# Two weight pieces beside each group of rows in a graph layer with a mixture of experts: where the pieces are loaded, split and read

## The reference, cut to what matters

```python
W = zeros((256, 256)).at[src, dst].set(edge_weight)      # the last edge with these indices wins
x = x + layernorm(x) @ W
xn = layernorm(layernorm(x)) * gamma + beta
logits = xn @ Wr + br                                    # 8 experts
w_full = softmax over the two largest logits, 0 elsewhere
for e in range(8):
    h = gelu(xn @ W1[e] + b1[e])                         # 256 -> 512
    y = y + (h @ W2[e] + b2[e]) * w_full[..., e]         # 512 -> 256
x = x + y
```

## Time and profile before

| what | us |
|---|---|
| three timed runs: lowest, median, highest | 1133.49, 1137.07, 1141.1 |
| the profiled execution, its own time | 1138.41 |
| its span in the profile (first to last recorded instruction) | 1136.7 |
| busy in the span: PE, DVE, ACT, POOL | 949.9, 759.6, 622.8, 590.5 |
| start of the first W2 load beside a group that waits (end of DVE's group 3) | 146.25 |
| first load of `zin` | 465.91 |

### The profile page before, as it was taken

One profiled execution on the slowest core, in us unless ns is written; L12 is line 12 of the kernel. 1 busy time (PEld: TensorE's weight loads), 2 busy tenths in 40 slices (PEclk: granted clock), 3 DMA queues, 4 the chain that ended last, 5 costly groups with the idle time before them and its releaser, 6 DMA issues. The chain is left out here.

```text
span 1136.7 us, 25491 instructions
## 1 busy us (share of the span) xinstructions
PE 949.9 (84%) x6852; PEld 896.3 (79%) x6853; DVE 759.6 (67%) x2345; ACT 622.8 (55%) x1309; POOL 590.5 (52%) x457
## 2 busy tenths in 40 slices
PE   2557876676667757699999999999999999999992
PEld 1236765565556547699999999999999999999992
DVE  6957856655555657377777777777777777777771
ACT  1025744434444442376676766766766766767661
POOL 3100664554545577044755566556556566565663
PEclk9886966666666665699999999999999999999997
DMA  3024444444444466544655455454454554554542
GB/s 93 1 70 103 160 161 140 147 145 140 165 142 149 159 217 194 173 78 82 93 88 91 76 93 89 78 93 84 83 93 80 88 93 75 93 89 79 93 72 32
DMA packets 96200, 121.45 MB, mean 107 GB/s; under 512 B 15240, under 2 KB 73776, under 8 KB 96028
## 3 DMA queue, kind: packets, MB, share of 16 engines
q0 software_dynamic: 39904, 53.56, 26.9%
q1 hardware_dynamic: 55944, 66.55, 19.7%
q10 hardware_dynamic: 308, 0.85, 0.2%
HBM read 51.93 MB, written 68.98 MB: 106 GB/s over the span
## 5 line engine op out<-in xcount | busy, mean ns | idle before, releaser
L565 POOL DMA_INDIRECT out_dram<-ysb,yid x210 | 379.5, 1807 | 295.8 <-ACT ysb L1342 141.8
L734 PE MATMUL psum<-xh,w1s 128*128 128x256 f32 x1680 | 311.6, 286 | 0.0
L549 POOL DMA_INDIRECT slots<-arena_z,pos x196 | 195.0, 995 | 222.0 <-DVE pos L1024 164.3
L734 PEld LDWEIGHTS psum<-xh,w1s 128*128 128x128 f32 x1680 | 257.7, 189 | 0.0
L747 PE MATMUL psum<-w2h,hl 128*128 x840 | 237.8, 283 | 0.0
L747 PE MATMUL psum<-w2l,hh 128*128 x840 | 237.5, 283 | 0.0
L747 PE MATMUL psum<-w2h,hh 128*128 x840 | 236.4, 281 | 0.0
L734 PE MATMUL psum<-xl,w1s 128*128 128x256 f32 x840 | 235.8, 281 | 0.0
L1161 DVE TENSOR_TENSOR hl<-hact,hh 128x512 fp32r<-128x512 f32 x210 | 145.6, 693 | 87.5 <-ACT hh L1214 87.5
L646 PE MATMUL psum<-table,arena_s 128*128 128x256 f32 x392 | 135.4, 504 | 60.5 <-DVE arena_s L1051 60.5
L1325 ACT ACTIVATE hact<-psum,b1T 128x256 f32<-128x256 f32 x420 | 174.6, 467 | 14.2 <-PE psum L734 2.7
(11 more groups left out here) (182 smaller groups left out, 1173.3 us busy)
## 6 DMA issues: line engine op xcount, KB each, us to landing
zin<-slots SPq DMA_DIRECT2D x105, 260.0 KB
arena_x<-in_x_dram SPq DMA_DIRECT2D x14, 512.0 KB, 6.0
out_dram<-arena_s SPq DMA_DIRECT2D x14, 512.0 KB, 4.5
wst_new<-in_L_ffn_W_dram SPq DMA_DIRECT2D x20, 256.0 KB, 3.1
arena_x<-in_x_dram SPq DMA_DIRECT2D x13, 384.0 KB, 7.0
out_dram<-arena_s SPq DMA_DIRECT2D x13, 384.0 KB
out_dram<-ysb,yid POOLq DMA_INDIRECT x210, 4.2
slots<-arena_z,pos POOLq DMA_INDIRECT x196, 2.6
```

The costliest lines, as they stand in the source:

```text
L549: pool.indirect_dma_start(slots[:, :], bass.IndirectOffsetOnAxis(ap=pos[b][0:n, k, s:s + 1], axis=0), zg[b][0:n, s, :], None).then_inc(sen ...
L565: pool.indirect_dma_start(out[:, :], bass.IndirectOffsetOnAxis(ap=yid[u % MB][:, n:n + 1], axis=0), ysb[u % YB][:, n, :], None, compute_op ...
L734: last = nc.tensor.matmul(bank[2 + 2 * b + q][:, m * PAIR:(m + 1) * PAIR], w1s[b][:, w, k, hb * P:(hb + 1) * P], xs[b][:, k * PAIR:(k + 1) ...
```

## The change

Two pieces stand beside each of the groups 2 to 13, so 24 beside groups and 8 behind the last one. In SP the two pieces of group g + 1 are loaded behind `turn_over(g)`, and their buffers' former users are the pieces of group g. In ACT the two `high` stand inside group g, between `exp_gap` and the z side. In DVE the two `low` of group g stand at its end. In PE the bias products of W1 pieces (groups 10 to 13) stand between the ranks and `edge_product(g, 1)`; five more come behind the last ranks and ahead of the count, and the last three behind `tables_ready`. The halves of each bias sum go to columns of their own in bank 6, and DVE adds both.

```diff
-BESIDE = 12
+BESIDE = 2 * (GROUPS - FIRST_BESIDE)
-MIDDLE = PIECES + WBUFS
+MIDDLE = BESIDE + WBUFS
+def beside(g):
+    return range(2 * (g - FIRST_BESIDE), 2 * (g - FIRST_BESIDE) + 2) if FIRST_BESIDE <= g < GROUPS else ()
...
 # SP
-            for n in range(2):
+            for n in beside(FIRST_BESIDE):
                 load_w(n)
             for g in range(2, GROUPS - 3):
                 turn_over(g, g % 2)
-                load_w(g)
+                for n in beside(g + 1):
+                    load_w(n)
             turn_over(GROUPS - 3, 1, full=False)
-            load_w(GROUPS - 3)
+            for n in beside(GROUPS - 2):
+                load_w(n)
             turn_over(GROUPS - 2, 0, load=False)
+            for n in beside(GROUPS - 1):
+                load_w(n)
             sp.wait_ge(xT_mm, NP * GROUPS)
-            for n in range(BESIDE, BESIDE + WBUFS):
+            for n in range(BESIDE, MIDDLE):
                 load_w(n)
...
 # PE
+            def bias(n):
+                e, k = (n - PIECES) // KD, n % KD
+                pe.wait_ge(stage_in[WBUF[n]], 16 * turn_of(n) + 16)
+                for hb in range(KH):
+                    at = G * E + E * KH * k + KH * e + hb
+                    last = nc.tensor.matmul(bank[6][:, at:at + 1], wst[WBUF[n]][:, hb * P:(hb + 1) * P], bet[:, k:k + 1], start=True, stop=True)
+                last.then_inc(w_read, 1)
...
                 if older:
                     ranks(g - 2)
+                for n in beside(g):
+                    if n >= PIECES:
+                        bias(n)
                 if x_side:
                     edge_product(g, 1)
...
             ranks(GROUPS - 1)
+            for n in range(BESIDE, MIDDLE):
+                bias(n)
             pe.wait_ge(routed, GROUPS)
...
-            for n in range(PIECES):
...
             pe.wait_ge(tables_ready, 1)
+            for n in range(MIDDLE, WHOLE):
+                bias(n)
...
 # DVE
-                if g > FIRST_BESIDE:
-                    low(g - FIRST_BESIDE - 1)
+                for n in beside(g):
+                    low(n)
...
-            for n in range(BESIDE - 1, MIDDLE):
+            for n in range(BESIDE, MIDDLE):
                 low(n)
...
-            v.tensor_tensor(b1T[:, :], bank[7][:, 0:E * KH], b1raw[:, :], ALU.add).then_inc(bias_ready, 1)
+            t.then(v.tensor_tensor(b1raw[:, :], bank[6][:, G * E:G * E + E * KH], b1raw[:, :], ALU.add))
+            v.tensor_tensor(b1T[:, :], bank[6][:, G * E + E * KH:G * E + 2 * E * KH], b1raw[:, :], ALU.add).then_inc(bias_ready, 1)
...
 # ACT
                 if older:
                     exp_gap(g - 2)
+                for n in beside(g):
+                    high(n)
                 if z_side:
...
                 group(g, g % 2)
-                high(g - FIRST_BESIDE)
```

More of the change, by code:

```diff
@@ L441, in _ @@
             sp.dma_start(out[(TILES - 1) * P:N, :], x1g[0:LAST, G - 1, :]).then_inc(x1_out[1], 16)
-            for n in range(BESIDE + WBUFS, WHOLE):
+            for n in range(MIDDLE, WHOLE):
                 load_w(n)
```

## The result

The changed kernel takes 1104.25 us (median of 4 runs, 1099.19 to 1108.13) beside 1139.09 us for the kernel before on the same chip (4 runs, 1133.49 to 1143.2). The ratio is 0.9686, 95% interval 0.9653 to 0.9719: 34.8 us faster, where 47 had been forecast. The profiled execution took 1105.56 us, its span is 1103.8 us.

A forecast was written before the change was run, and what follows sets the result against it. Loads of x queued on SP behind waiting weight loads were taken to bound the groups. 130.1 + 7 x 21.0 + 4 x 23.6 = 371.5, plus 47.0, puts `zin` at 418.5, 47.4 us earlier: 1091.0 us profiled, 1090 median, range 1062 to 1110.

The forecast's parts named there:

- the stall of x: Front-stage groups: DVE's 76.3 us wait for x, whose loads queue behind weight loads on SP, falls to under 10.
- R of group 2: R is when DVE finishes a group's router; for group 2, two high parts ahead of the z side give 130.1.
- z side begins (groups 3 to 9): ACT starts its z side after both high parts, 5.2 to 5.9 us behind the previous group's router end.
- cycle of groups 3 to 9: Weight wait, z-side chain of 14.2 us and clock loss: 21.0 us a group (19.4 to 22.7).
- cycle of groups 10 to 13: PE's W1 bias products ahead of `edge_product(g, 1)`, 1.75 us a piece, make 23.6 us a group.
- R of group 13 to `zin`: End of the front stage, from the last router's end through count, tables and fillers to the load of `zin`: 47.0 us.
- `zin` to the end: The pair stage, which the change does not touch, stays within 2 us of 668.
- Both signs asked for: DVE's wait for x under 10 us; ACT's z side 5.2 to 5.9 us behind the router's end.
- The clock: PE's z chain after its pause, groups 3 to 9: half clock costs 2.6 us; half of that, 1.3, was taken.
- a sign of being wrong: The forecast is wrong if, among other signs, cycles of groups 3 to 9 are under 19 or over 23 us.
- Weights that land late: Rival: weight loads compete with POOL's sends; at 10 us of landing the kernel takes 1163 us; slower had chance 0.05.
- Hidden weights: Rival: splits and POOL set the pace, 18.3 us for all eleven groups, 1050 us; hidden or nearly so, chance 0.12.

The follow-up runs named there:

- e1: The kernel before, with each weight load one group later on SP, behind the loads of x it had held up: 1052.28 us, ratio 0.9232.
- e2: The changed kernel with ACT's high parts moved from ahead of the z side to the end of its group: 1051.59 us, ratio 0.9234.
- e4: The changed kernel with five unused matmuls on PE ahead of the z transposes of groups 3 to 9: 1090.68 us, ratio 0.9567.
- e13: The changed kernel with an unused 128x112 tile declared last in the front stage, so no pair-stage tile moves: 1104.01 us, ratio 0.9694.
- e6: The changed kernel with the count put ahead of the five bias products behind the last group: 1106.58 us in one run.
- e3: e2 with PE's bias products also moved, behind the third piece of the z side and ahead of the last logits: 1051.02 us, ratio 0.9218.
- e11: The changed kernel with an unused 128x112 tile declared behind first_gelu, which moves pair-stage tiles: 1091.39 us, ratio 0.9558.
- e12: The kernel of e3 with the same unused tile in the same place as in e11: 1037.54 us, ratio 0.9106.
- e9: The kernel of e3 with a POOL memset of an otherwise unused tile behind each of 196 sends: 1052.4 us, ratio 0.9229.
- e10: The changed kernel with the same memset and tile as e9, behind each of POOL's 196 sends: 1090.11 us, ratio 0.9552.

## Why the prediction was right, and where it was off

The direction and the mechanism were right, and the range held the time, 6 us inside its upper end: the stall of x goes, ACT's wait for the weights takes its place, and the lost time shows in the front stage. The forecast gain was 12.6 us too large. The profiled execution took 1105.56 us against a sum of 1091.0, and the 14.6 us between them fall on these steps (spans add up to 14.5):

| Step | Predicted | Measured | Share of the error |
|---|---|---|---|
| R of group 2 | 130.1 | 131.32 | +1.2 |
| z side begins (groups 3 to 9) | R + 5.2 to 5.9 | R + 5.49 (mean of 7, 4.84 to 6.31) | 0 |
| cycle of groups 3 to 9 | 21.0 | 22.7 (mean of 7, 21.1 to 25.9) | +11.7 |
| cycle of groups 10 to 13 | 23.6 | 23.1 (mean of 4) | -2.1 |
| R of group 13 to `zin` | 47.0 | 46.8 | -0.2 |
| `zin` to the end | 670.8, as before | 674.7 | +3.9 |

**The stall and the new wait.** Both signs asked for are there: DVE's wait for x is gone and ACT's z side begins, in the mean, where it was put. e1 showed that the order of the queue was the cause of the stall, and e2 that the high parts ahead of the z side, with their wait and what hangs on it, were all that kept groups 3 to 9 of the changed kernel from 17 us. POOL waited 53.4 us in 12 times for its places after the first (136.3 less 82.9), 4.4 us a group, inside the 2 to 5 us forecast.

**The clock, the step that failed.** I took half of 2.6 us for the PE work behind the pause. In group 5 the time from the z side to `add(2)` is 192.01 - 183.61 = 8.4 us, where it was 5.6 in group 3 of before: 2.8 us, not 1.3. All seven products `edge_product(g, 2)` of groups 3 to 9 took 3.36 to 3.76 us; e4 filled the pause, brought four of seven back to 1.97 us, and got 13.6 us of the time back. In groups 4 to 9 it is 16.8 us in the mean from the z side to the next R, 2.6 more than the 14.2 of before (1.7 to 3.1 one by one): in the mean the full price. The Trainium skill (TensorE: Matmul & The Clock Gate, HAM oscillation) has a PE that waits for a DMA in every round of a loop start every round cold. By that rule the full price would have been the forecast, and the trace agrees, though PE waits here for ACT, and only ACT for the DMA. With 2.6 us in place of 1.3 the cycle is 22.3, and seven of them take up 9.1 of the 11.7 us. Two of the seven cycles, 25.9 and 23.2 us, are over the 23 that I had named as a sign of being wrong; their mean is not. The rest is group 3, with 25.9 us where the other six have 22.1 in the mean. Its loads left at 132.03 over 1.82 us, not 0.97, and its z side began only at 137.63, R + 6.3; more of it is the clock again, which was 0.50 from 140 to 157 us, so that all the rest of the group ran at 1.2 GHz (in group 5 it was 0.50 from 188.1 to 191.9 and 0.87 in the 3.1 us behind that). Why it stayed low so long there is open, and so is R of group 2, which came 1.2 us later than I had it and lies between 131.2 and 135.2 us in the seven executions with the high parts ahead of the z side.

**Groups 10 to 13.** 23.1 us against 23.6, and the steps came where they were put: `edge_product(g, 1)` ended 8.8, 11.3, 10.6 and 10.1 us behind R (forecast 9.7 to 11.2), and from there it was 12.8 to 13.1 us to the next R (12.7). But the price of the bias is the clock's. Group 13 in the timeline of PE:

```profile
362.64 2.96 PE L685 MATMUL psum<-bet,wst_new 128*128 128x1 f32 x16 [1.79 <-DMA wst_new<-in_L_ffn_W_dram]
...
365.46 3.76 PE L655 MATMUL psum<-table,arena_s 128*128 128x256 f32 x8
...
371.68 1.97 PE L655 MATMUL psum<-table,arena_s 128*128 128x256 f32 x8
```

The bias of a pair took 2.02 us in group 10 at a granted clock of 0.97, 3.58 us in group 11 at 0.50, and 3.43 and 2.96 us in groups 12 and 13. The product behind it took 3.43 to 3.76 us in all four, and `edge_product(g, 2)`, which is the slow one in groups 3 to 9, took 1.97 or 1.98. In e2 the same bias in the same place took 1.03 us a piece and the cycle 20.4 us. One sign failed: these cycles were to be 2 to 3 us longer than those of groups 3 to 9 and were only 0.4 us longer, because those had paid for the clock too.

**The end of the front stage** came out as it was added up: the count at R + 24.6 (forecast 25), the tables at R + 33.9 (34.5), `zin` at R + 46.8 (47.0).

**The pair stage** took 3.9 us more in the profiled execution, against a forecast of at most 2. It isn't the change: e13 and e6, which have the same pair stage, took 671.2 and 671.6 us from `zin` to the end. Most of it lies in the second layer's matmuls, which were busy for 714.3 us in all and 711.7 before (means of 281, 284 and 285 ns beside 281, 283 and 283), with their tiles in the same place. Why they differ between executions stays open.

**The rivals.** Weights that land late did not decide (landings of 3.4 us in the median for W2 and 6.4 at the longest, beside 3.1 and 6.4 before). Hidden weights were not what the change did. e1 and e2 reach the 1050 us which this rival gave: without ACT's wait the groups take 17.1 us, less than the 18.3 that I had for the splits and POOL, and what then sets the end is POOL, whose 14 sends take 18.2 us a group (255.4 / 14 in e3).

## What to carry to other kernels

A load whose buffer comes free late should never stand in an in-order queue ahead of a load that could go at once: moving it one place back was worth 85 us here, with no work changed. When a wait has been taken away, look at what the new order puts in front of the longest chain; here two high parts of 0.6 us, which stand as well at the end of ACT's group (e2), gave back 50 us because they wait for a DMA ahead of the z side, and because PE idles meanwhile and comes back at half clock. When three variants end at one time, look for an engine whose instructions follow each other without a break.

## What was not expected of the hardware

Where a tile lies in SBUF can set the rate of PE. The kernel passes `hh` and `hl` as the operand that is loaded into PE ahead of each matmul of the second layer (`LDWEIGHTS` of 128x128 on PEld), and `w2h` and `w2l` as the one that streams through it. With 448 bytes a partition ahead of them, `hh` and `hl` lie elsewhere while `w2h` and `w2l` stay, and these matmuls go from 281 to 285 ns to 276 ns (e11, e12, and the same in e9 and e10), with no effect when the tile is declared where it moves nothing of the pair stage (e13: 281 to 282 ns). In the first layer both operands moved, and its matmuls kept their 280 and 279 ns. Which of the tiles matters, and what decides between a good place and a bad one, was not tried; only one distance was.

The matmuls of the bias, with a single column (128x1), took 2.02 to 2.06 us for sixteen at a granted clock of 0.97 to 1.00 (group 10 of the changed kernel, group 11 of e2) and 3.58 us at 0.50 (group 11 of the changed kernel). A pause ahead of them does not tell which it will be: PE had waited 3.24 us ahead of the fast ones in group 10 and 2.69 us ahead of the slow ones in group 11.

A memset of 0.2 us between two indirect sends of POOL added 0.07 us: most of it fits between two sends.
